# A recommendation tower: interaction scratch with the quad outermost, stores as one run per row, and three edits of order

## The reference, cut to what matters

```
BATCH = 2048, 26 id fields, DIM = 128, dense features (2048, 128)
e        = 26 embedding rows per sample, tbl_f[ids[:, f]]        # 10 tables of 1000 rows, 16 larger ones
combined = concat([dense, e])                                    # (2048, 27, 128)
gram     = einsum('bfd,bgd->bfg', combined, combined)            # (2048, 27, 27)
h = concat([dense, gram's upper triangle (351), dense])          # (2048, 607)
h = relu(h @ W_top1 + b_top1)                                    # 512
h = relu(h @ W_top2 + b_top2)                                    # 256
y = h @ W_top3                                                   # (2048, 1)
```

## Time and profile before

| | |
|---|---|
| Median of three runs | 359.31 us |
| The profiled execution's own time | 359.83 us |
| Its span (first to last instruction) | 358.0 us |
| PE busy | 325.9 us (91%) |
| POOL busy (plus 0.3 us between two gathers) | 250.0 us (70%) |
| DVE busy | 240.7 us (67%) |
| ACT busy | 183.7 us (51%) |
| DMA packets | 48069, of them 26790 under 512 bytes |
| Mean granted TensorE clock | 0.986 |

### The profile page before, as it was taken

One profiled execution on the slowest core, in us unless ns is written; L12 is line 12 of the kernel. 1 busy time (PEld: TensorE's weight loads), 2 busy tenths in 40 slices (PEclk: granted clock), 3 DMA queues, 4 the chain that ended last, 5 costly groups with the idle time before them and its releaser, 6 DMA issues.

```text
span 358.0 us, 10391 instructions
## 1 busy us (share of the span) xinstructions
PE 325.9 (91%) x4192; PEld 312.3 (87%) x4192; DVE 240.7 (67%) x721; ACT 183.7 (51%) x360; POOL 250.0 (70%) x264
## 2 busy tenths in 40 slices
PE   0558789999999999999999999999999999999576
PEld 0548679989999998999899999999899999998565
DVE  3889987996469762995389654986299556951012
ACT  1345555556633763457534664557445664366224
POOL 5777777777777777777777777777777777775020
PEclk9987999999999999999999999999999999999989
DMA  5999657664447434662457444653356344421230
GB/s 146 235 249 246 157 160 193 158 168 133 99 101 181 115 76 103 139 170 69 99 120 187 95 82 106 149 149 69 103 131 185 82 98 102 125 68 46 34 78 0
DMA packets 48069, 44.80 MB, mean 125 GB/s; under 512 B 26790, under 2 KB 42150, under 8 KB 48022
## 3 DMA queue, kind: packets, MB, share of 16 engines
q1 hardware_dynamic: 38448, 26.89, 31.8%
q0 software_dynamic: 8320, 16.87, 19.5%
q10 hardware_dynamic: 1254, 0.39, 0.6%
HBM read 39.33 MB, written 4.78 MB: 123 GB/s over the span
## 4 chain that ended last, share of the span: by engine, by line
PE 81%; DVE 7%; DMA 6%; SPq 2%; ACT 2%; issue 1%; POOL 0%; ACTq 0%
PE ps_o L335 39%; PE ps_m L386 16%; PE ps_g L375 15%; PE ps_t L346 7%; DVE onehot L749 5%; DMA oh_ids<-onehot_ids 3%; DVE tbl_lo L734 2%; DMA interaction_scratch<-inter 2%; PE ps_m L416 2%; SPq L207 1%; DMA x<-interaction_scratch 1%; PE ps_g L446 1%; POOL interaction_scratch L190 0%; SPq L228 0%; ACT emb L555 0%
## 5 line engine op out<-in xcount | busy, mean ns | idle before, releaser
L313 POOL DMA_INDIRECT rows<-tables,idx x256 | 247.4, 966 | 80.4 <-issue 76.9
L749 DVE TENSOR_SCALAR onehot<-oh_ids,rownum 125x256 fp32r<-125x256 int32 x640 | 200.2, 388 | 50.9 <-PE ps_o L335 43.1
L335 PE MATMUL ps_o<-onehot,tbl_hi 125*128 125x256 f32 x640 | 163.9, 295 | 22.0 <-DVE tbl_lo L734 21.8
L335 PE MATMUL ps_o<-onehot,tbl_lo 125*128 125x256 f32 x640 | 159.0, 287 | 0.0
L335 PEld LDWEIGHTS ps_o<-onehot,tbl_hi 125*128 125x128 f32 x640 | 125.0, 195 | 27.3 <-DVE tbl_lo L734 23.3
L335 PEld LDWEIGHTS ps_o<-onehot,tbl_lo 125*128 125x128 f32 x640 | 125.4, 196 | 0.0
L555 ACT ACTIVATE emb<-ps_o 128x256 f32<-128x256 f32 x80 | 49.3, 740 | 87.0 <-PE ps_o L335 87.0
L375 PEld LDWEIGHTS ps_g<-emb 128*54 128x54 f32 x2048 | 53.6, 130 | 4.8 <-issue 1.8
L375 PE MATMUL ps_g<-emb 128*54 128x54 f32 x2048 | 56.0, 214 | 1.8 <-ACT emb L581 0.8
L571 ACT ACTIVATE emb<-ps_t 128x512 f32<-128x512 f32 x63 | 45.8, 729 | 9.9 <-PE ps_t L346 9.6
L595 ACT ACTIVATE inter<-ps_g 128x432 f32<-128x432 f32 x64 | 33.9, 532 | 15.6 <-PE ps_g L375 13.1
(11 more groups left out here) (60 smaller groups left out, 206.5 us busy)
## 6 DMA issues: line engine op xcount, KB each, us to landing
oh_ids<-onehot_ids SPq DMA_DIRECT2D x80, 128.0 KB
rows<-tables,idx POOLq DMA_INDIRECT x256, 2.4
x<-interaction_scratch SPq DMA_DIRECT2D x23, 117.0 KB
inter<-small_tables SPq DMA_DIRECT2D x4, 448.0 KB
interaction_scratch<-inter SPq DMA_DIRECT2D x30, 47.2 KB
x<-small_tables SPq DMA_DIRECT2D x3, 448.0 KB
h<-small_tables SPq DMA_DIRECT2D x3, 448.0 KB
interaction_scratch<-inter SPq DMA_DIRECT2D x32, 38.2 KB
```

Of the source, the lines that this page charges most:

```text
L313: pool.indirect_dma_start(rows[e][:, k, :], None, tables[k], bass.IndirectOffsetOnAxis(ap=idx[:, NG * hh + k:NG * hh + k + 1], axis=0),).t ...
L335: mm = pe.matmul(o, tbl[p][:, k, c, :], onehot[n % SLOTS_OH][:, c, :], start=(c + p == 0), stop=(c == TCHUNKS - 1 and p == 1))
L749: op = nc.vector.tensor_scalar(onehot[n % SLOTS_OH][:, c, :], oh_ids[0:TPART, n % IDS, :], rownum[:, c:c + 1], None, ALU.is_equal)
```

## The change

`scratch` becomes (q, f, g, 64 samples). A store of one quad then writes, for each of its rows f, one run of 21, 17, 8 or 13 entries of 256 bytes that are neighbours in DRAM. The load of a chunk can no longer be one DMA, since a pair's 256 samples lie in four places: `load_x` takes a list of quads and issues one DMA for each, with 117 runs of 256 bytes. Three other edits: `load_ids(2)` goes ahead of table 1 and `load_ids(3)` ahead of the identity; `layer2(m, 0)` of block 6 goes behind `grams(b)`; in the last block SP and ACT each store bands 0 and 1 and the wrapped part for two quads, each loads chunk 0 for two quads, and POOL's wait at line 318 goes.

```
-    scratch = nc.dram_tensor("interaction_scratch", (FEATURES, WRAP, QUAD, TB), f32,
+    scratch = nc.dram_tensor("interaction_scratch", (QUAD, FEATURES, WRAP, TB), f32,
-                eng.dma_start(scratch[f0:f1, f0 + 1:g1, q, :],
+                eng.dma_start(scratch[q, f0:f1, f0 + 1:g1, :],
-                eng.dma_start(scratch[f0:FEATURES, FEATURES:WRAP, q, :],
+                eng.dma_start(scratch[q, f0:FEATURES, FEATURES:WRAP, :],
-        def load_x(eng, i, c):
+        def load_x(eng, i, c, quads):
...
-            src = bass.AP(tensor=scratch.tensor, offset=(PAIR_F * c * (WRAP + 1) + 1) * BLOCK,
-                          ap=[[BLOCK, SHIFTS], [(WRAP + 1) * BLOCK, PAIR_F], [1, BLOCK]])
-            eng.dma_start(x[0:PAIR_ROWS, c, :], src).then_inc(x_loaded[c], 16)
+            for q in quads:
+                src = bass.AP(tensor=scratch.tensor, offset=((q * FEATURES + PAIR_F * c) * WRAP + PAIR_F * c + 1) * TB,
+                              ap=[[TB, SHIFTS], [(WRAP + 1) * TB, PAIR_F], [1, TB]])
+                eng.dma_start(x[0:PAIR_ROWS, c, TB * q:TB * (q + 1)], src).then_inc(x_loaded[c], 16)
...   (SP, every block)
-                    load_x(sp, i, c)
+                    load_x(sp, i, c, range(QUAD))
...   (SP, start)
             load_ids(1)
+            load_ids(2)
             load_stage(sp, 1)
-            load_ids(2)
+            load_ids(3)
             sp.dma_start(ident[:, :], identity).then_inc(ident_loaded, 16)
             load_stage(sp, 2)
             load_stage(sp, 3)
-            load_ids(3)
...   (SP, last block)
-            store_band(sp, LAST, 0, range(0, 2), inter_stored[0])
-            store_band(sp, LAST, 1, range(QUAD), inter_stored[1])
+            for b in range(2):
+                store_band(sp, LAST, b, range(0, 2), inter_stored[b])
+            store_wrapped(sp, LAST, range(0, 2))
+            load_x(sp, LAST, 0, range(0, 2))
             for c in range(1, PAIR_CHUNKS):
-                load_x(sp, LAST, c)
+                load_x(sp, LAST, c, range(QUAD))
...   (POOL, last block)
-            pool.wait_ge(inter_stored[0], 16 * QUAD * BLOCKS)
             store_band(pool, LAST, 2, range(QUAD), last_stored)
...   (PE, last_body)
-                layer2(m, 0)
                 last_transposes()
                 grams(b)
+                layer2(m, 0)
                 layer2(m, 1)
...   (ACT)
-                    act.wait_ge(x_loaded[c], 16 * (m + 1))
+                    act.wait_ge(x_loaded[c], 16 * (m + 1) * (1 if c == PAIR_CHUNKS else QUAD))
...
-                store_band(act, LAST, 0, range(2, QUAD), inter_stored[0])
-                store_wrapped(act, LAST, range(QUAD))
+                for b in range(2):
+                    store_band(act, LAST, b, range(2, QUAD), inter_stored[b])
+                store_wrapped(act, LAST, range(2, QUAD))
                 relus2(m)
-                load_x(act, LAST, 0)
+                load_x(act, LAST, 0, range(2, QUAD))
```

## The result

The changed kernel takes 362.16 us (median of five runs, 361.31 to 362.86) where the kernel before, timed beside it, takes 359.31: a ratio of 1.008, with a 95% interval of 1.0055 to 1.0105. It is slower, by 2.9 us. Forecast were 358.3 us and a range that ended at 361.0. The profiled execution of after has an own time of 361.31 us and a span of 359.5 us; before it was 359.83 and 358.0.

What follows compares the result with a forecast made beforehand. PE bounds the middle blocks, POOL's gathers pace the end, and the last turn through DRAM is exposed. Grams -1.2 and turn +0.2 give -1.0 us: median 358.3 us, likeliest 357.4 to 359.2, whole range 355.3 to 361.0.

Steps and rivals of the forecast that it cites:

- Ids: At the start, earlier ids let DVE win 1.9 us of a 2.73 us wait; PE earlier through all blocks, not the total.
- Layer 2 behind the grams: Before the last grams, 1.43 us of matmuls move behind them; grams start at 330.5, not 331.69: 1.2 us won.
- Loads of the last turn: Chunk loads take 0.83 us each to issue, eight on SP 6.6 us; each lands 2.4 us after its start.
- Rival 1: Last turn: short loads issue cheaply, 0.38 + 0.04 us each; 3.5 us won, 355.8 us; chance 0.13.
- rival 2: Last turn: SP's load queue becomes the bound, over 1.02 us a load; at 1.13 us, 361.0 us; chance 0.10.
- Rival 5: Stores: descriptors stay at 256 bytes, so the last load lands 2.6 us later than forecast, 360.9 us; chance 0.08.
- Rival 6: POOL's gathers, which pace the end: fewer packets spare POOL 2 us, giving 356.5 us; chance 0.05.
- if the last gather moves: Named sign of being wrong: POOL's last gather was to stay within 1 us of 327.3 us.
- Rival 3: Last turn: both queues share one generator, so chunk 0's four issues take 3.3 us, not 1.7; 359.9 us; chance 0.07.
- bands 1 and the wrapped part land by about 339.3: Last turn's stores: these land by about 339.3 us, and chunk 1's load waits until then.
- rival 4: Half clock falls on the last grams or layers: half of 3.4 us lost, 1.7 us, 360.0 us; chance 0.15.
- "Cost 0" for the middle blocks: Middle blocks: last chunk issued about 4 us later still lands before ACT takes it; DVE's idling covers later ids; no loss.

Runs made afterwards that it cites:

- Both order edits alone: Kernel before with only ids 2 and 3 ahead of the tables and block 6's layer 2 whole behind the last grams: 358.37 us, ratio 0.996.
- the repeated run: The changed kernel timed and profiled once more with no edit, against the kernel before: 362.36 us, ratio 1.0088.
- the shared loads: Changed kernel with the last turn's loads of chunks 1 and 2 split, SP quads 0 and 1, ACT quads 2 and 3: 358.36 us, ratio 0.996.
- the filled change: Changed kernel plus 14, 9 and 12 matmuls into an unread PSUM bank ahead of the last block's chunks 0, 1 and 2: 360.09 us, ratio 1.0016.
- the old layout with everything else: Old layout, one load per chunk, with both order edits, divided last stores, no POOL wait, and filling matmuls on PE: 357.65 us, ratio 0.9948.

## Why the prediction was wrong

What held, by the prediction's own steps:

- *Ids.* DVE's idle time for ids is gone, and the split of the first weights starts at 49.98 us where it started at 53.33: 3.4 us earlier, not 1.9. The startup's own stretch of half clock (before: 24.1 to 30.9 us) went too. At most one of the 3.4 us reached the total, since POOL paces the end: the ids alone gave 0.5 us by the medians.
- *Layer 2 behind the grams.* Forecast -1.2 with the grams at 330.5. Both order edits alone measured -1.1, and over the nine profiled kernels with both edits the median start of the grams is 330.56 (329.36 to 331.32). The one edit or the other gives it; they don't add.
- *Middle blocks from the third on.* Cost 0; a load's issue of 0.775 us there (forecast 0.79).
- *Loads of the last turn.* Eight at a pitch of 0.82 us (forecast 0.83), the last one landing 2.23 us after its start (forecast 2.4). Rival 1 (cheap short loads) and rival 2 (over 1.02 us) are both refuted by L220:

```profile
L220 SPq DMA_DIRECT2D x<-interaction_scratch x94: 771/774/1436, 67.7 to 345.9; - x94
L220 ACTq DMA_DIRECT2D x<-interaction_scratch x2: 844/883/922, 337.1 to 338.0; - x2
```

- *Rival 5* is refuted by the packets and by band 0 at T + 3.6. *Rival 6*, that POOL moves, is not borne out: the last gather goes out between 325.95 and 327.50 us in all profiles, new layout or old. The first profile after has the earliest, 1.3 us ahead of before, so the sign "if the last gather moves" came up in it, and did not in the repeated run. *Rival 3* is refuted by the shared loads. The Trainium skill (Perfetto Trace Analysis, "DMA Instruction — HWDGE") has the generator locked while it makes descriptors; if the whole 0.77 us were locked, two queues would have stood at 1.5 us for a load, and they stood at 0.77 to 0.83. Another section of that page, "DMA Optimizations", advises to spread DMAs over several issuing engines where making descriptors is the bottleneck, and the 2.6 us of the shared loads agree.

What failed, first: **the term "bands 1 and the wrapped part land by about 339.3", T + 4.8.** They landed at T + 6.64. The SP and ACT queues' last turn:

```profile
333.42 2.12 SPq L190 DMA_DIRECT2D interaction_scratch<-inter  x4
333.42 2.12 ACTq L190 DMA_DIRECT2D interaction_scratch<-inter  x4
...
333.68 2.14 POOL L190 DMA_DIRECT2D interaction_scratch<-inter  x4 [6.79 <-ACT inter L596]
...
335.58 0.98 SPq L199 DMA_DIRECT2D interaction_scratch<-inter  x2
335.58 1.00 ACTq L199 DMA_DIRECT2D interaction_scratch<-inter  x2
```

The prediction gives no working for T + 4.8; with six issues of 0.37 the last store would start at T + 1.9, which leaves it 2.9 us to land. Two things were off. Six stores took 3.14 us to issue, 0.52 each and not 0.37, so the last one starts at T + 2.55: 0.6 us. The 0.37 was taken from one queue that issues alone in the middle blocks; here SP and ACT issue side by side. (POOL is not the reason: without its stores the six take 3.1 us as well.) And the last store needed 4.08 us to land and not 2.9: 1.2 us. That is what POOL's four stores cost. The prediction lets them run beside the others, since their wait goes, and puts what they do to bands 0 and 1 and the wrapped part at nothing. Left out, the last store lands in 3.04 us; with POOL still waiting, in 2.88. So the edit that was to help, POOL's wait taken away, delays the landing on which eight loads hang.

The turn grew by 1.95 where I had +0.2; of the 1.75 between, +1.8 is this term, and -0.17 the quicker landing of the load. Band 0 too landed at T + 3.6 and not T + 2.9, outside its own bounds of 0.6 us, but nothing on the chain waited for it. The stores were to give back some 5 us, from T + 10.04 to T + 4.8. They gave back 3.4, and of these the long runs are only 0.8 (T + 7.14 with short runs, T + 6.37 with long ones); the rest is that POOL no longer comes last and that the stores are divided.

Second: **rival 4, the clock, had 0.15 and decides.** Its price was 1.7 us, for half clock over 3.4 us; 2.3 us were measured (2.0 at the end by the spans), out of a stretch of 10.2. My argument against it was that no full 4.5 us of idling stands before work that counts. That took the one idle stretch that the earlier trace rows show as the least that is needed. In after PE is not idle but works 1.86 of 3.40 us and 1.65 of 2.30 (fences above), chunk by chunk, and the clock fell; with PE filled it did not. The fourfold load makes these pauses long: it spreads the three chunks to 3.2 and 3.4 us apart (2.0 and 2.6 before), where PE is busy 1.65 us with each. What I can't settle is when it falls: the profiled run without POOL's stores had much the same pauses (1.07 and 1.49 us, against 2.19 and 1.49 in after and 1.28 and 2.23 in the repeated run) and kept the full clock, while six others of its ten runs were at a mean clock of 0.981 to 0.986.

Third: **"Cost 0" for the middle blocks** failed in the first of them. PE waited 0.88 us for x and the block took 1.6 us more, in the profile of every kernel with the new layout (41.4 to 42.1 us, or 43.7 and 44.0 where the clock fell behind the wait, against 40.1 to 40.6 with the old one). This is the sign of being wrong that the prediction named itself. The ids' lead of 3.4 us covered it; that was luck, for the two were not set against each other. The layout alone, without that lead, has its T 0.8 us later than before.

By the ledger: -1.35 (T) + 1.85 (turn) + 2.0 (end) = +2.5 us for the repeated change against -1.0 forecast. With the landing at T + 4.8 and the clock held it would be -1.2. The difference of the first two profiles, 1.5 us, understates the loss of 2.9: the profiled execution of after, 361.31, is the fastest of its five runs and 0.85 us under their median, and that of before lay 0.5 above its own. The spread between runs I can't lay to a stage.

## What to carry to other kernels

In an exposed round trip through DRAM count the DMA issues on the last queue first: this one paid 0.82 us for each load however short, and dividing the same loads between two queues brought back more than the whole change had lost (4.0 us, part of it through the clock). Take a row of issue or landing only from a stretch with as many queues and bytes in flight as the one you forecast, and when an edit lets one more queue start at once, ask whose landing it delays. Look at the first turn of a loop by itself: a middle block read later in the trace said nothing of the one that waited. And where work will come in pieces with pauses between them, price the half clock over all that follows the pauses, not only over an idle stretch like the one that the old trace happens to show.

## What the runs showed of the hardware

- A load of 117 runs takes 0.77 us to issue with runs of 256 bytes and 0.79 with runs of 1024 bytes, so it is not the bytes that are paid. It is not the number of runs alone either: ids of 128 rows take 0.38, and the first store of the last turn on SP is issued in 0.28 us with 189 runs (before) and in 0.28 with nine (after). What makes the 0.77 stays open.
- Two queues that issue such loads side by side take 0.77 to 0.83 us for each, one alone 0.77. Six stores on each of two queues side by side take 0.52 us each, twelve on one queue alone 0.38.
- A load of a quarter of the bytes in 256-byte runs lands 2.23 us after its start, one with 1024-byte runs after 2.71. The rule of the Trainium skill (DMA: Bandwidth & Descriptors, "Specifications") that under 512 bytes a transfer is off line rate does not show in this landing; as many bytes in longer runs were not tried.
- Stores of nine or 13 long runs (9 or 13, not 72 to 189) land 0.8 to 1.1 us sooner after T, though the last of them starts 1.4 us sooner (T + 2.56 and T + 3.95, the filled change and the old layout with everything else).
- Four stores of 18 KB on a third queue, started with the others, delay the last landing by 0.8 to 1.1 us.
- PE busy for 3.5 us in the 5.7 us up to 343.7 was followed by 10.2 us at 1.2 GHz in the change, and 3.4 of 5.7 us up to 344.9 in the repeated run likewise; 3.5 of 5.7 us up to 344.9, in the run without POOL's stores, was followed by the full clock.
